# Box-filter layer: all shifted rows copied between the layers, its rings moved, sums and fixes reordered

## The chip, the cores and the metric

The kernel runs on one core of a Trainium2 chip. The metric is the time of one execution on the device in microseconds (us), the median over several executions.

## What is computed

The input is 8 images of 16 channels and 512 x 512 pixels (float32). Two residual layers follow each other; `_gn` normalises over groups of two channels.

```python
# layer 0
x = x + _L0_conv_ref(_gn(x), w_real, w_imag, b_real, b_imag)   # rfftn, 3x3 complex convolution over the spectrum, irfftn
# layer 1
x = x + _L1_conv_ref(_gn(x))                                   # mean filter 15 x 15, zero padding
```

## The kernel before

One image lies in SBUF as `img`, 128 partitions x 64 rows x 512 pixels. A partition holds one channel (16) and one block of 64 neighbouring rows (8 blocks), so `T` is 64 and step `u` or `t` of a loop treats one row of every block at once. The images follow each other; for each, layer 0 runs over 64 steps, a gap of a few us follows in which the statistics of layer 0's result are made (`statistics`: BN_AGGR, two tiny matmuls, square root, then a chain of one-column operations in `sc`), and then layer 1 runs over 64 steps, storing its rows and loading those of the next image. From step 16 on (`follow`, `LAG`) layer 1 also counts and sums the rows of the next image; the last image has nothing to follow.

Layer 1 filters 15 rows by a running sum. POOL writes the difference of the entering and the leaving row (`difference`, L1490), ACT scales it (`scale_row`, L946 or L947), PE turns it by a transposition that accumulates nothing (`turn_step`, L759), ACT and DVE split the turned row into two float16 parts (`high_part` L812, `low_part` L1343), PE multiplies them with a band matrix that adds into one PSUM bank (`box_row`, L770), and DVE adds the bank to the image row (`add_box`, L1351) into `ob_all`, which has three buffers of two rows. SP stores a buffer (L371); `add_box` of an even row waits until the store that used the buffer three pairs earlier has landed. The first filter row is made from `head` and `tail` (`turn_first`): `tail` is the sum of the last rows of each block, added up by POOL (`presum`, L1442 and L1445), scaled by DVE (L1356) after the statistics.

The blocks lie in different partitions, so the rows across a block's edge have to be moved between partitions by DMA on SP's queue, seven rows before a block (`rows_before`) and seven after it (`rows_after`). Before, both sets share the pieces 4 to 10 of one buffer, `arena`: the rows before are copied in the gap, the rows after, in two parts, in layer 1 itself, behind the stores of pair 0 and pair 2. The differences of steps 8 to 56 go through a ring of three rows (`diff`), the float16 parts through another (`parts`), both in `arena` too. POOL's first difference waits for `tail_ready`, the scaled tail.

At the end of layer 0, POOL finishes row 63's two additions (`add_terms`, L1430 and L1433), DVE adds them to the image (`finish_row`, L1281, then BN_STATS, L1284), ACT makes the half mean (L878) and adds it to the row (L888), and DVE corrects all 64 row means in one operation (L1334) before BN_AGGR (L1122).

Each engine works through its own program in order; the order is written by hand and held by semaphores. The wait of `add_box` for a store is this:

```python
if u % 2 == 0:
    dve.wait_ge(stored[j % NS], PRIMED + 32 * (b * USES[j % NS] + j // NS))
```

Of the kernel before, what the change touches and what calls it, by code (L numbers as in the profile page):

```python
# [32 lines left out]
F16 = mybir.dt.float16  # L33
# [128 lines left out]
def build(nc, x, w_real, w_imag, b_real, b_imag, tab, bd_dram, out):  # L162
    x_v = x.rearrange("b c (s hl t) w -> b s c hl (t w)", s=2, hl=HL)
    out_v = out.rearrange("b c (s hl t) w -> b s c hl (t w)", s=2, hl=HL)
    with ExitStack() as ctx:
# [21 lines left out]
        diff = [piece[s] for s in (0, 1, 11)]  # L187
        parts = [piece[s].bitcast(F16).rearrange("p (l k m) -> p l k m", l=2, k=NQ) for s in (2, 3, 12)]
        head, tail = piece[14], piece[15]
        across = [piece[4 + r] for r in range(R)]  # L190
        across_all = arena[:, 4 * W:(4 + R) * W]

        def diff_row(u):
            return across[u - 1] if u <= R else diff[u % 3] if u < T - R else across[u - (T - R)]
# [24 lines left out]
        wrap_row = sb("wrap_row", [P, W], F16)  # L219
        wrap_high = sb("wrap_high", [P, W], F16)  # L220
        block_mat = sb("block_mat", [P, 9, P])
        kappa = sb("kappa", [P, 3, T, 2])
        bias_c = sb("bias_c", [P, 2, T, 2])
# [65 lines left out]
        before_in, after_in = [[sem(f"{name}{s}") for s in range(2)] for name in ("before_in", "after_in")]  # L289
# [52 lines left out]
        def _(sp):  # L342
# [93 lines left out]
            def rows_before(b):  # L436

                def shifted(first, rows, signal):
                    to, at = across_all[:, first * W:(first + rows) * W], T - R + first
                    of = img[:, at:at + rows, :].rearrange("p t w -> p (t w)")  # L440
# [4 lines left out]
                sp.dma_start(across_all[0:HP:HL], tab["no_row"]).then_inc(before_in[0], 16)  # L445
                sp.wait_ge(x1_whole, (b + 1) * T - 3)
                shifted(0, 4, before_in[0])
                sp.wait_ge(x1_whole, (b + 1) * T)
                shifted(4, 3, before_in[1])

            def rows_after(b, part):

                first, rows = ((0, CHUNK), (CHUNK, R - CHUNK))[part]
                to = across_all[:, first * W:(first + rows) * W]
                of = img[:, first:first + rows, :].rearrange("p t w -> p (t w)")
                sp.wait_ge(turned, b * T + first + rows + 1)
                for hl in range(HL - 1):
                    sp.dma_start(to[hl:P:HL], of[hl + 1:P:HL]).then_inc(after_in[part], 16)
                sp.dma_start(to[HL - 1:HP:HL], of[HP:P:HL]).then_inc(after_in[part], 16)
                sp.dma_start(to[HP + HL - 1:P:HL], tab["no_row"][:, 0:rows * W]).then_inc(after_in[part], 16)  # L460

            with sp.Fori(0, B - 1) as b:
                matrices(b)
                rows_before(b)
                for j in range(T // 2):
# [4 lines left out]
                    if j in (0, 2):  # L470
                        rows_after(b, j // 2)
# [1061 lines left out]
```

## Time and profile before

| | |
|---|---|
| median of 3 runs | 3462.5 us (3455.91 to 3465.9) |
| the profiled execution's own time | 3468.07 us |
| its span, first to last instruction | 3466.0 us |
| mean granted TensorE clock | 0.978 |
| busy: PE, DVE, POOL, ACT | 89%, 89%, 78%, 71% |
| DMA | 573.59 MB, mean 165 GB/s |

PE and DVE are both busy for nine tenths of the span, so an idle stretch of either is a place where the other, or a DMA, is waited for. An image takes 414 us, some 130 us of them in layer 1.

### The profile page before, as it was taken

Reading aid. Unit: us, or ns where it says so; the run is one execution under the profiler, and the core shown is the slowest. Engines: PE = TensorE matmul, PEld = TensorE weight load, DVE = VectorE, ACT = ScalarE, POOL = GpSimd, SP = SyncE. Lnnn points to the kernel's source line nnn. Section 1 sums busy time; section 2 is a strip of 40 time slices with the busy share of each in tenths; the row PEclk is TensorE's granted clock in tenths of the full one; section 3 lists DMA queues with packets and bytes.
Section 4 is the critical chain, followed back from the end, with each engine's and each line's share of the span. In section 5 each row is a group of like instructions: output and inputs, shape, how many; then the busy total and the mean of one; then the engine's idle time right before and its main releaser. Section 6 shows DMA issues by size and latency. Waiting matters only on the chain.

```text
span 3466.0 us, 112555 instructions
## 1 busy us (share of the span) xinstructions
PE 3085.5 (89%) x36064; PEld 1877.5 (54%) x36064; DVE 3077.9 (89%) x6018; ACT 2447.4 (71%) x4742; POOL 2713.3 (78%) x2231
## 2 busy tenths in 40 slices
PE   2299979999889998899899998999989999889986
PEld 1155555555555555555555555555555555555555
DVE  7789978999889989899798997989978998889987
ACT  2568865787658876588666886578865887658876
POOL 5069975899749987599876997589974998749986
PEclk9599999999999999999999999999999999999999
DMA  8656668666776659766596666966678665877655
GB/s 206 202 87 131 129 202 257 114 128 124 241 214 128 127 119 288 170 127 129 155 288 130 130 128 188 276 110 128 121 230 227 122 127 118 261 194 130 127 130 176
DMA packets 726766, 573.59 MB, mean 165 GB/s; under 512 B 592416, under 2 KB 667776, under 8 KB 712064
## 3 DMA queue, kind: packets, MB, share of 16 engines
q1 hardware_dynamic: 704000, 451.67, 56.0%
q10 hardware_dynamic: 22400, 117.46, 13.2%
q8 instruction: 178, 2.92, 0.4%
q14 instruction: 188, 1.54, 0.2%
HBM read 262.08 MB, written 148.90 MB: 119 GB/s over the span
## 4 chain that ended last, share of the span: by engine, by line
PE 43%; DVE 19%; issue 14%; POOL 10%; SPq 7%; DMA 5%; ACT 1%; ACTq 1%; DVEq 1%; POOLq 0%
PE p L626 19%; PE h_ps L536 7%; PE h_odd L536 7%; DVE ob_all L1351 5%; POOL arena L1490 4%; SPq L417 3%; DVE arena L1343 3%; PE p L770 3%; DMA out<-ob_all 3%; PE h_ps L626 2%; DVE stat L1104 2%; POOL ob_all L1433 2%; DVE ob_all L1272 2%; PE p L633 2%; POOL ob_all L1430 2%
## 5 line engine op out<-in xcount | busy, mean ns | idle before, releaser
L626 PE MATMUL p<-arena,bd_all 64*64 64x512 f16 x16896 | 1263.2, 380 | 25.3 <-DVE ob_all L1266 14.2
L626 PEld LDWEIGHTS p<-arena,bd_all 64*64 64x64 f16 x16896 | 556.4, 105 | 435.2 <-issue 281.8
L1430 POOL TENSOR_TENSOR ob_all<-ob_all,img 128x512 f32<-128x512 f32 x512 | 663.6, 1296 | 60.0 <-DVE ob_all L1266 55.3
L1433 POOL TENSOR_TENSOR ob_all<-ob_all 128x512 f32<-128x512 f32 x512 | 653.4, 1276 | 40.1
L1490 POOL TENSOR_TENSOR arena<-img 128x512 f32<-128x512 f32 x392 | 498.3, 1273 | 176.5 <-PE h_ps L759 97.5
L888 ACT ACTIVATE img<-img,half_row (+1 forms) x1024 | 489.0, 531 | 5.1 <-ACT half_row L878 0.4
L770 PE MATMUL p<-band,arena 128*128 128x135 f16 (+1 forms) x4096 | 341.8, 228 | 151.7 <-DVE ob_all L1351 146.2
L1266 DVE SCALAR_TENSOR_TENSOR ob_all<-p,bias_c,cosw 128x256 f32<-128x256 f32 x1024 | 445.9, 477 | 22.3 <-PE p L626 9.1
L1272 DVE SCALAR_TENSOR_TENSOR ob_all<-p,bias_c,cosw 128x256 f32<-128x256 f32 x1024 | 443.8, 475 | 0.0
L1423 POOL TENSOR_TENSOR arena<-arena 128x512 f16<-128x512 f32 x256 | 309.2, 1208 | 162.0 <-ACT arena L862 162.0
L861 ACT ACTIVATE arena<-img,sc 128x512 f16 (+1 forms) x512 | 435.2, 850 | 0.0
L946 ACT ACTIVATE arena<-arena,sc 128x512 f32<-128x512 f32 x392 | 282.8, 721 | 210.0 <-POOL arena L1490 196.2
L1351 DVE SCALAR_TENSOR_TENSOR ob_all<-p,img 128x512 f32<-128x512 f32 x512 | 348.1, 680 | 86.2 <-PE p L770 52.2
L1284 DVE BATCH_NORM_STATS2 stat<-img (+1 forms) x512 | 355.6, 695 | 58.6
L770 PEld LDWEIGHTS p<-band,arena 128*128 128x128 f16 x4096 | 261.9, 99 | 256.3 <-issue 241.7
L536 PE MATMUL h_ps<-hilbert,arena 128*128 128x256 f16 x3072 | 380.0, 274 | 7.1 <-DMA arena<-arena 7.0
L575 PE MATMUL p<-img,bd_all 128*64 128x256 f32 x2048 | 301.9, 404 | 92.5 <-POOL bd_all L1394 66.5
L536 PE MATMUL h_odd<-hilbert,xT_more 128*128 128x256 f16 x3072 | 379.8, 273 | 1.0 <-DMA xT_more<-arena 0.7
L536 PEld LDWEIGHTS h_ps<-hilbert,arena 128*128 128x128 f16 x3072 | 280.2, 98 | 139.8 <-issue 99.4
L536 PEld LDWEIGHTS h_odd<-hilbert,xT_more 128*128 128x128 f16 x3072 | 279.9, 98 | 137.7 <-issue 96.4
L1423 POOL TENSOR_TENSOR arena<-g_more,arena 128x512 f16<-128x512 f32 x256 | 307.5, 1201 | 58.3 <-ACT g_more L862 38.2
L1104 DVE BATCH_NORM_STATS2 stat<-img 128x6 f32<-128x512 f32 x512 | 335.4, 681 | 3.0 <-DMA img<-in_x 1.7
(182 smaller groups left out, 5191.5 us busy)
## 6 DMA issues: line engine op xcount, KB each, us to landing
out<-ob_all SPq DMA_DIRECT2D x512, 256.0 KB, 4.7
bd_all<-bd_dram SPq DMA_DIRECT2D x512, 224.0 KB, 2.5
img<-in_x ACTq DMA_DIRECT2D x168, 512.0 KB, 6.9
img<-in_x ACTq DMA_DIRECT2D x112, 256.0 KB, 5.3
img<-in_x SPq DMA_DIRECT2D x24, 512.0 KB, 25.7
arena<-img SPq DMA_DIRECT2D x48, 256.0 KB, 3.3
arena<-img SPq DMA_DIRECT2D x48, 192.0 KB, 2.6
bd_dram<-ob_all SPq DMA_DIRECT2D x11, 768.0 KB, 3.6
```

The source lines that it names most:

```text
L536: m = mm(dst(a), row[:, 4 * lx + k, :], tb["hilbert16"][:, lt, k, 0:cols], start=(half == 0 and i == 0), stop=(half == 1 and i == 2))
L626: m = mm(bank[out_half * HP:(out_half + 1) * HP, :], bd[s % RB][rows, 6 * lm + (j if own else j + 1), :], part, start=opens and i3 == 0, s ...
L770: m = mm(p0[0][:, lo:hi], parts[u % 3][:, l, k, :], tb["band16"][:, lo - k * P + R:hi - k * P + R], start=(u == 0 and k == 0 and l == 0), ...
L861: nc.scalar.activation(halves(gp[s][:, 0, :]), row, ACT.Identity, bias=sc[:, 9:10], scale=sc[:, 8:9])
L888: ins = nc.scalar.activation(row, row, ACT.Identity, bias=half_row[:, s, a:a + 1])
L1266: ins = V.scalar_tensor_tensor(t1[:, a, :], p1[:, a * HALF:(a + 1) * HALF], bias_c[:, 1, t, 1 - a:2 - a], cosw[:, a, :], ALU.subtract, ALU ...
L1272: ins = V.scalar_tensor_tensor(t2[:, a, :], p2[:, a * HALF:(a + 1) * HALF], bias_c[:, 0, t, 1 - a:2 - a], sinw[:, a, :], ALU.add, ALU.mult)
L1351: V.scalar_tensor_tensor(ob[j % NS][:, u % 2, :], p0[0], 1.0 / (K * K * BOX_SCALE), img[:, u, :], ALU.mult, ALU.add).then_inc(row_out, 1)
L1423: G.tensor_tensor(gp[s][:, 1, :], g32[s % 2], gp[s][:, 0, :], ALU.subtract).then_inc(g_split, 1)
L1430: G.tensor_tensor(q, term_row[s % 2][0], parity(img[:, t, :]), ALU.add).then_inc(first_added, 1)
L1433: G.tensor_tensor(q, q, term_row[s % 2][1], ALU.add).then_inc(q_done, 1)
L1490: G.tensor_tensor(diff_row(u), more, less, ALU.subtract).then_inc(moved, 1)
```

## The change

All 14 shifted rows are now copied in the gap between the layers (`rows_across`): the rows before to pieces 0 to 6 of `arena`, the rows after to pieces 7 to 13. The rings of differences and of parts move out of `arena` into buffers that layer 0 uses: `g32_more`, `xT_more`, `wrap_rows`, a joint buffer of `kappa` and `bias_c`, and `bd_all`. POOL's first difference no longer waits for the scaled tail. POOL adds `presum` of row 60 behind row 63's additions. DVE corrects the means of rows 0 to 59 ahead of `finish_row` of row 63, and those of the last four behind it. Four SCALAR_TENSOR_TENSOR operations on one column in `statistics` become TENSOR_SCALAR with a column as scalar. ACT's `high_part(0)` stands ahead of `scale_row(2)`.

```diff
--- before.py
+++ after.py
@@ -184,14 +184,11 @@
...
 
-        diff = [piece[s] for s in (0, 1, 11)]
-        parts = [piece[s].bitcast(F16).rearrange("p (l k m) -> p l k m", l=2, k=NQ) for s in (2, 3, 12)]
         head, tail = piece[14], piece[15]
-        across = [piece[4 + r] for r in range(R)]
-        across_all = arena[:, 4 * W:(4 + R) * W]
+        rows_of_before, rows_of_after = arena[:, 0:R * W], arena[:, R * W:2 * R * W]
 
         def diff_row(u):
-            return across[u - 1] if u <= R else diff[u % 3] if u < T - R else across[u - (T - R)]
+            return piece[u - 1] if u <= R else diff[u % 3] if u < T - R else piece[R + u - (T - R)]
 
...
@@ -216,11 +213,16 @@
...
-        kappa = sb("kappa", [P, 3, T, 2])
-        bias_c = sb("bias_c", [P, 2, T, 2])
+        biases = sb("biases", [P, 5 * 2 * T])
+        kappa = biases[:, 0:6 * T].rearrange("p (f t a) -> p f t a", f=3, a=2)
+        bias_c = biases[:, 6 * T:10 * T].rearrange("p (f t a) -> p f t a", f=2, a=2)
+        flat16 = bd_all[:].rearrange("p s r -> p (s r)")
+        diff = [g32_more[:], xT_more[:], biases[:, 0:W]]
+        parts = [row.rearrange("p (l k m) -> p l k m", l=2, k=NQ)
+                 for row in (flat16[:, 0:2 * W], flat16[:, 4 * W:6 * W], wrap_rows[:])]
...
@@ -433,51 +435,43 @@
...
-            def rows_before(b):
+            def rows_across(b):
+
+                def rows_of(first, rows):
+                    return img[:, first:first + rows, :].rearrange("p t w -> p (t w)")
 
                 def shifted(first, rows, signal):
-                    to, at = across_all[:, first * W:(first + rows) * W], T - R + first
-                    of = img[:, at:at + rows, :].rearrange("p t w -> p (t w)")
+                    to, of = rows_of_before[:, first * W:(first + rows) * W], rows_of(T - R + first, rows)
                     for hl in range(HL - 1):
                         sp.dma_start(to[hl + 1:P:HL], of[hl:P:HL]).then_inc(signal, 16)
                     sp.dma_start(to[HP:P:HL], of[HL - 1:HP:HL]).then_inc(signal, 16)
                 sp.wait_ge(p0_ready, (b + 1) * T + PRIMED)
-                sp.dma_start(across_all[0:HP:HL], tab["no_row"]).then_inc(before_in[0], 16)
+                sp.dma_start(rows_of_before[0:HP:HL], tab["no_row"]).then_inc(before_in[0], 16)
                 sp.wait_ge(x1_whole, (b + 1) * T - 3)
                 shifted(0, 4, before_in[0])
+                to, of = rows_of_after, rows_of(0, R)
+                for hl in range(HL - 1):
+                    sp.dma_start(to[hl:P:HL], of[hl + 1:P:HL]).then_inc(after_in, 16)
                 sp.wait_ge(x1_whole, (b + 1) * T)
                 shifted(4, 3, before_in[1])
-
-            def rows_after(b, part):
-
-                first, rows = ((0, CHUNK), (CHUNK, R - CHUNK))[part]
-                to = across_all[:, first * W:(first + rows) * W]
-                of = img[:, first:first + rows, :].rearrange("p t w -> p (t w)")
-                sp.wait_ge(turned, b * T + first + rows + 1)
-                for hl in range(HL - 1):
-                    sp.dma_start(to[hl:P:HL], of[hl + 1:P:HL]).then_inc(after_in[part], 16)
-                sp.dma_start(to[HL - 1:HP:HL], of[HP:P:HL]).then_inc(after_in[part], 16)
-                sp.dma_start(to[HP + HL - 1:P:HL], tab["no_row"][:, 0:rows * W]).then_inc(after_in[part], 16)
+                sp.dma_start(to[HL - 1:HP:HL], of[HP:P:HL]).then_inc(after_in, 16)
+                sp.dma_start(to[HP + HL - 1:P:HL], tab["no_row"]).then_inc(after_in, 16)
 
             with sp.Fori(0, B - 1) as b:
                 matrices(b)
-                rows_before(b)
+                rows_across(b)
...
                     store(b, j, j % NS)
-                    if j in (0, 2):
-                        rows_after(b, j // 2)
                     if j == 4:
                         sp.wait_ge(turned, b * T + 1)
                         sp.dma_start(tail, tab["hilbert_kernel"]).then_inc(bias_in, 16)
             matrices(B - 1)
-            rows_before(B - 1)
+            rows_across(B - 1)
             for j in range(T // 2):
                 store(B - 1, j, j % NS)
-                if j in (0, 2):
-                    rows_after(B - 1, j // 2)
             for s in range(NS):
                 sp.wait_ge(stored[s], PRIMED + 32 * B * USES[s])
 
@@ -961,15 +955,15 @@
...
                 scale_row(1)
+                high_part(0)
                 scale_row(2)
-                high_part(0)
                 def load_next(t, rows, signal):
 
                     act.wait_ge(row_out, PRIMED + b * T + t + rows)
                     if t + rows + R <= NDIFF:
                         act.wait_ge(moved, b * NDIFF + t + rows + R)
                     if t < R:
-                        act.wait_ge(after_in[t // CHUNK], (b + 1) * (16 * COPIES))
+                        act.wait_ge(after_in, (b + 1) * (16 * COPIES))
...
@@ -1124,18 +1118,17 @@
                 dve.wait_ge(s_mean, n)
                 V.tensor_copy(sc[:, 6:7], c_ps[:, 16:17])
                 lk(V.tensor_tensor(sc[:, 2:3], sc[:, 0:1], c_ps[:, 16:17], ALU.subtract))
-                V.scalar_tensor_tensor(sc[:, 3:4], sc[:, 2:3], sc[:, 2:3], sc[:, 1:2],
-                                       ALU.mult, ALU.add).then_inc(s_dev, 1)
+                V.tensor_scalar(sc[:, 3:4], sc[:, 2:3], sc[:, 2:3], sc[:, 1:2], ALU.mult, ALU.add).then_inc(s_dev, 1)
                 dve.wait_ge(s_gvar, n)
                 V.tensor_scalar(sc[:, 4:5], c_ps[:, 17:18], EPS, None, ALU.add).then_inc(s_var, 1)
                 dve.wait_ge(s_sd, n)
                 dve.wait_ge(s_var, n)
                 lk(V.reciprocal(sc[:, 7:8], sc[:, 5:6]))
 
-                lk(V.scalar_tensor_tensor(sc[:, 11:12], sc[:, 7:8], sc[:, 7:8], sc[:, 4:5], ALU.mult, ALU.mult))
+                lk(V.tensor_scalar(sc[:, 11:12], sc[:, 7:8], sc[:, 7:8], sc[:, 4:5], ALU.mult, ALU.mult))
                 lk(V.tensor_scalar(sc[:, 11:12], sc[:, 11:12], -0.5, 1.5, ALU.mult, ALU.add))
-                lk(V.scalar_tensor_tensor(sc[:, 8:9], sc[:, 7:8], ROW_SCALE, sc[:, 11:12], ALU.mult, ALU.mult))
-                shift = V.scalar_tensor_tensor(sc[:, 9:10], sc[:, 8:9], -1.0, sc[:, 6:7], ALU.mult, ALU.mult)
+                lk(V.tensor_scalar(sc[:, 8:9], sc[:, 7:8], ROW_SCALE, sc[:, 11:12], ALU.mult, ALU.mult))
+                shift = V.tensor_scalar(sc[:, 9:10], sc[:, 8:9], -1.0, sc[:, 6:7], ALU.mult, ALU.mult)
...
@@ -1328,11 +1321,16 @@
...
                 wave_terms(b * T + T - 1, T - 1, (T - 1) % NG, T // NG)
-                for t in (T - 2, T - 1):
-                    finish_row(b * T + t, t, t % NG, T // NG)
-                dve.wait_ge(half_made, (b + 1) * T)
-                V.scalar_tensor_tensor(parity_mean, parity_mean, 0.5, known[:], ALU.mult, ALU.add).then_inc(stat_fixed, 1)
-                dve.wait_ge(stat_fixed, b + 1)
+                def fix_means(first, end):
+
+                    dve.wait_ge(half_made, b * T + end)
+                    V.scalar_tensor_tensor(parity_mean[:, first:end], parity_mean[:, first:end], 0.5,
+                                           known[:, first:end], ALU.mult, ALU.add).then_inc(stat_fixed, 1)
+                finish_row(b * T + T - 2, T - 2, (T - 2) % NG, T // NG)
+                fix_means(0, T - 4)
+                finish_row(b * T + T - 1, T - 1, (T - 1) % NG, T // NG)
+                fix_means(T - 4, T)
+                dve.wait_ge(stat_fixed, 2 * b + 2)
                 statistics(b * 2 + 2, b, False)
 
...
@@ -1466,9 +1464,8 @@
                         slot(i, s, 1)
                 for t in range(T - NG, T):
                     slot(t // NG, t % NG, t // NG, sum_t=t - 4 if t - 4 >= T - R else None)
-                presum(b * T + T - 4, T - 4)
                 add_terms(b * T + T - 1, T - 1, (T - 1) % NG, T // NG)
-                for t in range(T - 3, T):
+                for t in range(T - 4, T):
                     presum(b * T + t, t)
 
...
@@ -1485,11 +1482,10 @@
                             pool.wait_ge(turned, b * T + u - 2)
                         more, less = img[:, u + R, :], img[:, u - R - 1, :]
                     else:
-                        pool.wait_ge(after_in[0 if u - (T - R) < CHUNK else 1], (b + 1) * (16 * COPIES))
+                        pool.wait_ge(after_in, (b + 1) * (16 * COPIES))
                         more, less = diff_row(u), img[:, u - R - 1, :]
                     G.tensor_tensor(diff_row(u), more, less, ALU.subtract).then_inc(moved, 1)
 
-                pool.wait_ge(tail_ready, b + 1)
                 for u in range(1, T):
                     difference(u)
                     if follow and u >= LAG + 2 and (u - (LAG + 2)) % CHUNK == 0:
```

What stands on SP's queue (between the fetches of layer 0's matrices, L407 before and L409 after, and the stores of layer 1, L371 and L373). Before:

```order
L445 DMA arena<-tab_no_row 16x3584
L442 DMA arena<-img 32x2048 x3
L443 DMA arena<-img 16x2048
L442 DMA arena<-img 32x1536 x3
L443 DMA arena<-img 16x1536
L371 ISA
L371 DMA out<-ob_all 16x4x1024
L371 ISA
L371 DMA out<-ob_all 16x4x1024
L458 DMA arena<-img 32x2048 x3
L459 DMA arena<-img 16x2048
L460 DMA arena<-tab_no_row 16x2048
```

And now:

```order
L449 DMA arena<-tab_no_row 16x3584
L446 DMA arena<-img 32x2048 x3
L447 DMA arena<-img 16x2048
L454 DMA arena<-img 32x3584 x3
L446 DMA arena<-img 32x1536 x3
L447 DMA arena<-img 16x1536
L457 DMA arena<-img 16x3584
L458 DMA arena<-tab_no_row 16x3584
L373 ISA
L373 DMA out<-ob_all 16x4x1024
L373 ISA
L373 DMA out<-ob_all 16x4x1024
```

The rows after a block (L458 to L460 before, L454, L457 and L458 now) stand ahead of the first store instead of between the stores, and three of them stand ahead of the second part of the rows before.

POOL at the end of layer 0 (`add_terms` of rows 62 and 63 and the presums of rows 59 to 63; `arena` is the tail). Before:

```order
L1430 TENSOR_TENSOR ob_all<-ob_all,img 128x512
L1433 TENSOR_TENSOR ob_all<-ob_all 128x512
L1444 ISA
L1445 TENSOR_TENSOR arena<-arena,img 128x512
L1444 REGISTER_ALU
L1445 TENSOR_TENSOR arena<-arena,img 128x512
L1429 REGISTER_ALU
L1430 TENSOR_TENSOR ob_all<-ob_all,img 128x512
L1433 TENSOR_TENSOR ob_all<-ob_all 128x512
```

And now:

```order
L1428 TENSOR_TENSOR ob_all<-ob_all,img 128x512
L1431 TENSOR_TENSOR ob_all<-ob_all 128x512
L1442 ISA
L1443 TENSOR_TENSOR arena<-arena,img 128x512
L1427 REGISTER_ALU
L1428 TENSOR_TENSOR ob_all<-ob_all,img 128x512
L1431 TENSOR_TENSOR ob_all<-ob_all 128x512
```

One presum has moved from ahead of row 63's two additions to behind them.

ACT at the start of layer 1 (the scaled head, then scaled differences 1, 2, 3 and the high parts 0 and 1). Before:

```order
L947 ACTIVATE arena<-arena,sc 128x512
L951 ISA
L947 ACTIVATE arena<-arena,edge_bias,sc 128x512
L951 REGISTER_ALU
L947 ACTIVATE arena<-arena,edge_bias,sc 128x512
L812 ACTIVATE arena<-h_ps 128x512
L951 REGISTER_ALU
L947 ACTIVATE arena<-arena,edge_bias,sc 128x512
L812 ACTIVATE arena<-h_ps 128x512
```

And now:

```order
L941 ACTIVATE arena<-arena,sc 128x512
L945 ISA
L941 ACTIVATE arena<-arena,edge_bias,sc 128x512
L806 ACTIVATE bd_all<-h_ps 128x512
L945 REGISTER_ALU
L941 ACTIVATE arena<-arena,edge_bias,sc 128x512
L945 REGISTER_ALU
L941 ACTIVATE arena<-arena,edge_bias,sc 128x512
L806 ACTIVATE bd_all<-h_ps 128x512
```

Two scalings instead of one stand between high part 0 and high part 1.

## Rows read from the trace of the kernel before

**Rows 1.** Waits of DVE, whole run: us in total, times, longest.

```profile
DVE ob_all L1351 <- DMA out<-ob_all: 33.9, 15, 5.2
```

**Rows 2.** Timeline of DVE, L1351: start, us, operation, [idle before <- releaser].

```profile
464.97 0.68 DVE L1351 SCALAR_TENSOR_TENSOR ob_all<-p,img 128x512 f32<-128x512 f32 x1
...
482.08 0.69 DVE L1351 SCALAR_TENSOR_TENSOR ob_all<-p,img 128x512 f32<-128x512 f32 x1 [0.23 <-PE p L770]
...
487.62 0.69 DVE L1351 SCALAR_TENSOR_TENSOR ob_all<-p,img 128x512 f32<-128x512 f32 x1 [4.24 <-DMA out<-ob_all]
...
494.95 0.67 DVE L1351 SCALAR_TENSOR_TENSOR ob_all<-p,img 128x512 f32<-128x512 f32 x1
...
2966.76 0.69 DVE L1351 SCALAR_TENSOR_TENSOR ob_all<-p,img 128x512 f32<-128x512 f32 x1 [0.24 <-PE p L770]
...
2981.07 0.67 DVE L1351 SCALAR_TENSOR_TENSOR ob_all<-p,img 128x512 f32<-128x512 f32 x1
...
3381.74 0.69 DVE L1351 SCALAR_TENSOR_TENSOR ob_all<-p,img 128x512 f32<-128x512 f32 x1 [0.53 <-DMA out<-ob_all]
```

**Rows 3.** Timeline, DMA issues of SP and of ACT in the first layer 1.

```profile
475.25 2.50 SPq L458 DMA_DIRECT2D arena<-img  x3
...
479.21 4.04 SPq L371 DMA_DIRECT2D out<-ob_all  x4
...
478.09 0.70 ACTq L974 DMA_DIRECT2D img<-in_x  x1
```

**Rows 4.** Windows: stretch, us, busy us of PE, PEld, DVE, ACT, POOL, PEclk, DMA share, GB/s.

```profile
502.00:552.00 50.00, 49.99 (x450) 31.15 (x448) 50.00 (x85) 33.65 (x56) 39.31 (x36) 1.00 1.00 292
```

**Rows 5.** DMA issues from 500 to 556 us: count, KB each, median us to landing.

```profile
out<-ob_all SPq DMA_DIRECT2D x32, 256.0 KB, 5.8
```

**Rows 6.** Timeline of the first gap, from layer 0's last rows to layer 1's first.

```profile
445.15 2.64 POOL L1445 TENSOR_TENSOR arena<-arena,img 128x512 f32<-128x512 f32 x2
...
447.75 1.29 POOL L1430 TENSOR_TENSOR ob_all<-ob_all,img 128x512 f32<-128x512 f32 x1
...
449.12 1.27 POOL L1433 TENSOR_TENSOR ob_all<-ob_all 128x512 f32<-128x512 f32 x1
...
450.42 0.75 DVE L1281 SCALAR_TENSOR_TENSOR img<-p,sc,ob_all 128x512 f32<-128x512 f32 x1 [2.37 <-POOL ob_all L1433]
...
452.44 0.69 DVE L1334 SCALAR_TENSOR_TENSOR stat<-stat,known 128x128 f32<-128x128 f32 x1 [0.55 <-ACT half_row L878]
...
453.18 1.88 DVE L1122 BATCH_NORM_AGGREGATE sc<-stat 128x2 f32<-128x384 f32 x1
...
458.13 0.22 DVE L1145 TENSOR_SCALAR edge_bias<-ends,sc 128x2 f32<-128x2 f32 x1
458.25 0.15 DVE L1146 TENSOR_SCALAR sc<-sc 128x1 f32<-128x1 f32 x1
...
458.57 0.55 DVE L1356 TENSOR_SCALAR arena<-arena,sc 128x512 f32<-128x512 f32 x1
459.28 8.66 POOL L1490 TENSOR_TENSOR arena<-img,arena 128x512 f32<-128x512 f32 x7 [4.38 <-DVE arena L1356]
459.47 0.38 PE L749 MATMUL h_ps<-ident,arena 128*128 128x128 f32 x2
...
462.53 0.58 ACT L812 ACTIVATE arena<-h_ps 128x512 f16<-128x512 f32 x1
...
463.76 0.57 ACT L812 ACTIVATE arena<-h_ps 128x512 f16<-128x512 f32 x1
```

**Rows 7.** DVE's L1210 beside POOL: one pair in the timeline, and the line's ns min/median/max.

```profile
605.44 1.16 POOL L1423 TENSOR_TENSOR arena<-g_more,arena 128x512 f16<-128x512 f32 x1 [2.97 <-DVE img L1204]
605.51 1.11 DVE L1210 TENSOR_SCALAR edge<-edge,sc 128x2 f32<-128x2 f32 x1
...
L1210 DVE TENSOR_SCALAR edge<-edge,sc x8: 228/666/1111, 189.8 to 3091.5; 128x2 f32<-128x2 f32 x8
```

**Rows 8.** The page's DMA issues: count, KB each, median us to landing.

```profile
arena<-img SPq DMA_DIRECT2D x48, 256.0 KB, 3.3
```

More of the change, by code:

```diff
@@ L218, in build @@
         xT = [row.bitcast(F16).rearrange("p (k m) -> p k m", k=8) for row in (piece[9], xT_more[:])]
-        wrap_row = sb("wrap_row", [P, W], F16)
-        wrap_high = sb("wrap_high", [P, W], F16)
+        wrap_rows = sb("wrap_rows", [P, 2 * W], F16)
+        wrap_row, wrap_high = wrap_rows[:, 0:W], wrap_rows[:, W:2 * W]
         block_mat = sb("block_mat", [P, 9, P])
-        kappa = sb("kappa", [P, 3, T, 2])
-        bias_c = sb("bias_c", [P, 2, T, 2])
+        biases = sb("biases", [P, 5 * 2 * T])
[5 more added lines that the diff above has]
+                 for row in (flat16[:, 0:2 * W], flat16[:, 4 * W:6 * W], wrap_rows[:])]
         known = sb("known", [P, T, 2])
@@ L288, in build @@
         scaled_row = sem("scaled_row")
-        before_in, after_in = [[sem(f"{name}{s}") for s in range(2)] for name in ("before_in", "after_in")]
+        before_in, after_in = [sem(f"before_in{s}") for s in range(2)], sem("after_in")
         turned, high_done, low_done, banded = sem("turned"), sem("high_done"), sem("low_done"), sem("banded")
@@ L914, in image @@
                 act.wait_ge(v_stacked, b + 1)
-                nc.scalar.activation(wrap_high[:], p0[2], ACT.Identity, scale=sc[:, 27:28]).then_inc(v_high, 1)
+                nc.scalar.activation(wrap_high, p0[2], ACT.Identity, scale=sc[:, 27:28]).then_inc(v_high, 1)
                 def slot(i, s, first):
@@ L1228, in layer0 @@
                 dve.wait_ge(c_made, b + 1)
-                V.tensor_copy(bias_c[:], c_tab[:, 0:2])
+                V.tensor_copy(bias_c, c_tab[:, 0:2])
                 lk(V.scalar_tensor_tensor(known[:], c_tab[:, 2], unscale, parity_mean, ALU.mult, ALU.add))
@@ L1233, in layer0 @@
                 dve.wait_ge(v_high, b + 1)
-                V.scalar_tensor_tensor(wrap_row[:], p0[2], sc[:, 26:27], wrap_high[:],
+                V.scalar_tensor_tensor(wrap_row, p0[2], sc[:, 26:27], wrap_high,
                                        ALU.mult, ALU.subtract).then_inc(v_wrap, 1)
```

## The prediction

> **What bounds the kernel now.** I read the waits of DVE first, because in layer 1 DVE adds every row and everything else follows its row count. The reader is to see one line there [rows 1]: `add_box` waited 33.9 us in the whole run for a store to land. Then I read where this happens, from the starts of `add_box` [rows 2]. Rows 0 to 11 of the first layer 1 take 482.08 - 464.97 = 17.11 us, 1.555 us a row. Row 12 then starts 5.54 us behind row 11 instead of 1.6, and its bracket says that it waited 4.24 us for `out<-ob_all`. The queues say why [rows 3]: row 12 reuses the buffer of pair 3. That pair was complete when row 7 was, near 476.5, but its store was issued at 479.21, behind the five copies of `rows_after`, part 2, that begin at 475.25; and the first 1 MB load of the next image enters the DMA engines at 478.09. From step 16 on, with the next image's rows counted and summed, PE and DVE are both busy for all of 50 us [rows 4]: there the row takes three DVE operations, no DMA is waited for though the engines move 292 GB/s, and nothing of this change reaches it. The third view is the gap between the layers [rows 6], a single chain from POOL's last additions over DVE's statistics to the first high part.
>
> **The stores' stall.** From row 11 to row 16 the first image takes 494.95 - 482.08 = 12.87 us [rows 2]. Without a wait it would take four steps of 1.555 and one of 1.80, since step 16 has a third DVE operation (three of 0.6): 8.02 us. The excess is 4.85 us: 4.24 of wait, the rest in the slower rows behind it. Seven images have a next image to load, and of the seven the first has the smallest excess and the seventh, with 2981.07 - 2966.76 = 14.31 us, the largest, 6.3. Between them lie 13.80, 12.91, 13.08, 12.88 and 13.00; together the seven excesses make 36.7 us. The eighth image has the same copies and no loads, and waited 0.53 us of which 0.24 is its ordinary pause [rows 2]: 0.3 us. So copies and loads together make the stall, neither the copies alone. The change takes 1.75 MB of copies out of this stretch, and with them the 2.7 us by which store 3 was late. What then stands between store 3 and its landing is the first load. Store and load demand 2 MB in 6.2 us here, 320 to 340 GB/s, more than the 292 of the steady stretch, where a store lands in 5.8 us [rows 4, 5]. The time allowed is from the second issue of a pair's store to the row that reuses it: five rows less 0.7 for the add and 1.4 for the issues, 7.8 - 2.1 = 5.7 us. That is even with 5.8, so I leave a remainder: between 0 and the half of the wait, 2.5 us an image, I take 0.5, as the burst lasts only five rows. Gain: 37.0 - 7 x 0.5 = 33.5 us.
>
> **The gap, ahead of the statistics.** Row 63's additions start directly behind the presum of row 59, at 445.15 + 2.64 / 2 = 446.47, instead of 447.75 [rows 6]: 1.28 us earlier. L1433 then ends at 449.11 and `finish_row` of row 63 could start there instead of at 450.42. But the new correction of 60 means stands in front of it and reads two SBUF operands while POOL works. What such an operation does is seen beside another operation of POOL [rows 7]: L1210, two columns of arithmetic, takes 0.228 us at best and 1.11 here, and 605.51 + 1.11 = 606.62 is where POOL's operation ends, 605.44 + 1.16 = 606.60. It waits until POOL's operation is over. The correction so ends some 0.15 us behind L1433 (an estimate between 0.02 of that pair and the 0.69 of L1334), and `finish_row` starts at 449.29, 1.13 us earlier. Its old successor L1334 came 2.02 us after it; the small correction of four means is due then, at 451.31, and again waits for the presum that POOL is at. POOL's operations follow each other by (8.66 - 1.27) / 6 = 1.23 us [rows 6]; from 449.29 the second ends at 451.8. BN_AGGR starts at 451.97 instead of 453.18: 1.2 us gained.
>
> **The gap, under POOL's differences.** Before, POOL stood idle for 4.38 us until the tail was scaled [rows 6], so no DVE operation of the statistics ever met it. Now presums run to 454.3 and differences 1, 2, 3, 4 start at 454.3, 455.55, 456.8 and 458.05. The four operations on one column cost 0.06 us more each, the difference between a TENSOR_SCALAR with a column as scalar and one without (0.22 against 0.15) [rows 6]: 0.24. L1145, two columns and of exactly L1210's form, is then due at 458.13 - 1.2 + 0.24 = 457.17, in difference 3, waits until 458.05 and ends at 458.23; before it ended at 458.35. The scaled tail L1356 is due at 458.45, in difference 4, and waits until 459.4; it ends near 459.85 where it ended at 459.12. `turn_first` starts 0.73 later than 459.47 and lasts 1.97, so high part 0 can start at 462.17, 0.36 earlier than 462.53. Behind it now stand two scalings instead of one. High to high was 463.76 - 462.53 = 1.23 with one; I take 0.72 for another, so high part 1 starts 1.95 later, at 464.12, 0.36 later than before. The first `add_box` waits for low part 1, so the rows start 0.36 us later: 8 x 0.36 = +2.9 us. Bounds: with no wait for POOL in the statistics the rows would start 1.3 us earlier (-10.6); with a further full operation of 1.23 us they would start 1.6 later (+12.8). I take the computed value, since every wait was placed by its own phase; L1145 would have to come 0.37 us earlier to slip in ahead of difference 3.
>
> The input's statistics run the same four operations, with POOL idle: 8 x 0.24 = +1.9 us.
>
> The Trainium skill, GPSIMD Engine Reference, section 1 (Specifications), says that POOL's SBUF interfaces are shared with VectorE, with contention for VectorE instructions in a two-port mode or with two SBUF inputs. By that rule L1145, L1356 and the corrections wait, and the trace agrees for L1210 (1.11 against 0.228 us). One-column TENSOR_SCALARs would not, if they have nothing to split; no row here shows one beside a busy POOL, and the sum takes them at their idle price.
>
> **The copies in the gap.** They cost nothing by my reckoning, and what hides them is this. The first four rows before lie in front of them on the queue. Three copies of 448 KB follow, then, from 452.2 on, the three other rows before: 1.4 MB and 0.7 MB. A 256 KB copy lands 3.3 us after issue [rows 8]; at the steady 292 GB/s [rows 4] the 2.1 MB take 7.2 us from about 451, so they land near 458.5. Difference 5 needs them at 459.3. If they are later, POOL waits, but scaled difference 5 is not needed by `turn_step` before 467; the cover is 6 to 7 us, and the cost beyond it is one for one. The last two copies, 0.44 MB, are needed at difference 57 and by the first load.
>
> **Sum.** 3468.07 - 33.5 + 2.9 + 1.9 = 3439.4 us for a profiled execution. The one of before stood 5.6 us above its median of 3462.5, so 3433.8; I say 3433.
>
> **The rivals.** First, no waits for POOL in the statistics, or lucky phases: everything else equal, -10.6 instead of +2.9, 3420 us. For it: L1334 in the old gap did pass POOL with only 0.69 us. Against: L1210 [rows 7]. 15%.
>
> Second, the stall is the loads' and not the copies'. Then half of it stays, say 16.5 us: 3450. For it: the burst demands more than the steady stretch, and 5.7 us allowed against 5.8 to land is no margin [rows 5]. Against: in the steady stretch itself no store is waited for, and store 3 was 2.7 us late by the copies alone [rows 3]. 13%.
>
> Third, slower than before. The one-column operations also wait for POOL. The five operations from L1135 to the first of the group with L1145 each wait for the one before, so each would catch POOL's next boundary: 5 x 1.23 = 6.2 us instead of 1.2 of their own, and 0.8 for L1127, 5.8 us an image, 46 us: 3479. It decides above 3.6 us an image, three operations that wait. For it: nothing in the trace shows a one-column operation beside a busy POOL that passes unhindered. Against: they have one tensor operand of one element, and the operations of layer 1 that read one operand from SBUF keep their 0.68 us while POOL works [rows 2]. The Trainium skill, VectorE: DVE Perf Modes, section Mode 2x_2P, says the two-port mode splits an operand in halves; one column has none, which speaks against this rival. 8%.
>
> The forecast keeps 60%; 4% is left for what I have not seen.
>
> **How the numbers follow.** 0.3% is 10 us, about what a measurement here can tell from no change, so faster means under 3452. The forecast and the first rival are faster, 75%, and of the second, centred at 3450, two thirds, 9%: 84%. Same is the other third of the second and half of the unseen, with rounding 8%; slower the third rival, 8%. The range runs from the first rival with a whole stall gained, 3412, to the second, 3452; outside are the third rival and the tails. The forecast's own range, 3424 to 3442, comes from the remainder of the stall (0 to 1.5 us an image) and a shift of the gap by half a POOL operation.
>
> **What would show it.** `add_box`'s wait for `out<-ob_all` falls from 33.9 to under 5 us, and row 11 to row 16 takes 8 to 8.6 us in every image. POOL's first difference starts near 454 and L1145 lasts near 1 us, L1356 over 1 us instead of 0.55. BN_AGGR starts 1.2 us sooner after the last matmul of layer 0, the first `add_box` at about the old time. The prediction is wrong if the wait on the stores stays above 15 us, if one-column TENSOR_SCALARs of the statistics last over 0.5 us in the gap, or if the steady rows change their 1.79 us.

## The result, and the profile after

The changed kernel takes 3433.1 us in the median of 7 runs (3431.01 to 3445.7) against 3462.5 (3455.91 to 3467.77): ratio 0.9927, 95% interval 0.991 to 0.9944. The forecast was 3433. Its profiled execution took 3433.1 us, span 3431.1, 35 us less than the one of before.

The waits of DVE, whole run, of the changed kernel (us in total, times, longest), beside [rows 1]:

```profile
DVE ob_all L1349 <- DMA out<-ob_all: 12.8, 19, 1.6
```

The stores' wait has fallen from 33.9 us to 12.8, but it has not gone. The timeline of DVE in the first layer 1 (start, us, operation, idle before) shows where it is now, beside [rows 2]:

```profile
481.25 0.69 DVE L1349 SCALAR_TENSOR_TENSOR ob_all<-p,img 128x512 f32<-128x512 f32 x1 [0.16 <-PE p L764]
...
482.84 0.69 DVE L1349 SCALAR_TENSOR_TENSOR ob_all<-p,img 128x512 f32<-128x512 f32 x1 [0.31 <-PE p L764]
...
486.46 0.69 DVE L1349 SCALAR_TENSOR_TENSOR ob_all<-p,img 128x512 f32<-128x512 f32 x1 [0.81 <-DMA out<-ob_all]
...
489.79 0.67 DVE L1349 SCALAR_TENSOR_TENSOR ob_all<-p,img 128x512 f32<-128x512 f32 x1
```

Row 12 (482.84) no longer waits; row 14 does, 0.81 us. Row 11 to row 16 takes 8.54 us where it took 12.87. The windows of this layer 1 (stretch, us, busy us of PE, PEld, DVE, ACT, POOL, PEclk, DMA share, GB/s) show that the DMA traffic now comes later, with the loads; from 469 to 475 us the kernel before moved 310 GB/s:

```profile
469.00:475.00 6.00, 4.12 (x48) 3.35 (x47) 4.93 (x8) 4.21 (x7) 2.37 (x2) 1.00 0.55 165
...
481.00:487.00 6.00, 3.91 (x44) 3.04 (x41) 4.48 (x8) 4.69 (x8) 5.40 (x6) 1.00 0.98 322
487.00:493.00 6.00, 4.56 (x50) 3.39 (x50) 5.76 (x11) 4.19 (x8) 4.26 (x5) 1.00 1.02 328
```

In the kernel before, the six us that begin in the stall read:

```profile
487.00:493.00 6.00, 4.15 (x33) 3.60 (x34) 3.87 (x6) 2.37 (x4) 2.10 (x2) 0.72 1.03 344
```

The granted clock (PEclk) of that stretch was 0.72 of full speed, so part of it ran at the lower level; from 481.9 to 487.5 PE had been busy for 1.67 of 5.6 us. Now it is 1.00. Rows 12 and 13 of the kernel before took 1.97 and 2.04 us, and the additions behind them waited 0.68 and 0.75 us for PE; in the eighth image, which has no such stall, the same rows took 1.53 and 1.59. So the old stall cost more than its wait.

The timeline of the gap, beside [rows 6]:

```profile
447.07 1.27 POOL L1431 TENSOR_TENSOR ob_all<-ob_all 128x512 f32<-128x512 f32 x1
447.27 1.23 DVE L1327 SCALAR_TENSOR_TENSOR stat<-stat,known 128x120 f32<-128x120 f32 x1
...
448.40 0.74 DVE L1274 SCALAR_TENSOR_TENSOR img<-p,sc,ob_all 128x512 f32<-128x512 f32 x1
...
451.02 1.88 DVE L1116 BATCH_NORM_AGGREGATE sc<-stat 128x2 f32<-128x384 f32 x1
...
453.59 8.80 POOL L1487 TENSOR_TENSOR arena<-img,arena 128x512 f32<-128x512 f32 x7
453.63 0.27 DVE L1121 TENSOR_SCALAR sc<-sc 128x1 f32<-128x1 f32 x1
...
456.14 1.19 DVE L1138 TENSOR_SCALAR edge_bias<-ends,sc 128x2 f32<-128x2 f32 x1
...
457.55 1.26 DVE L1354 TENSOR_SCALAR arena<-arena,sc 128x512 f32<-128x512 f32 x1
...
461.02 0.60 ACT L806 ACTIVATE bd_all<-h_ps 128x512 f16<-128x512 f32 x1 [2.02 <-PE h_ps L744]
461.52 1.51 ACT L941 ACTIVATE arena<-arena,edge_bias,sc 128x512 f32<-128x512 f32 x2
462.93 0.58 ACT L806 ACTIVATE bd_all<-h_ps 128x512 f16<-128x512 f32 x1
```

Three things are to be seen. POOL's seven differences run back to back from 453.59, so neither part of the shifted rows was late. Two DVE operations beside them, L1138 and L1354, last 1.19 and 1.26 us where the same lasted 0.22 and 0.55 (L1145 and L1356, [rows 6]), while L1121, on one column, lasts 0.27, as it does in the input's statistics with POOL idle. And ACT stands idle for 2.02 us ahead of high part 0 and then needs two scalings before high part 1.

From the starts of BN_AGGR, `finish_row` and `add_box` in the two timelines, summed over the eight images (one profile of each kernel):

| stretch, us | before | after | difference |
|---|---|---|---|
| input's BN_AGGR to row 0 of layer 0 | 259.8 | 254.1 | -5.7 |
| rows 0 to 62 of layer 0 | 1894.3 | 1892.3 | -1.9 |
| row 62 to row 63 | 30.7 | 20.1 | -10.6 |
| row 63 to BN_AGGR | 22.2 | 21.0 | -1.1 |
| BN_AGGR to first row of layer 1 | 95.4 | 105.1 | +9.8 |
| rows 0 to 11 | 136.9 | 136.8 | -0.1 |
| rows 11 to 16 | 100.9 | 70.9 | -30.0 |
| rows 16 to 32 | 225.5 | 229.8 | +4.3 |
| rows 32 to 63, and to the next BN_AGGR | 522.4 | 522.2 | -0.2 |

### The profile page after: what moved, and what is told of

Its sections match the earlier page's. It is cut to its first block, busy times and chain, and to the rows that moved or that the text cites. A ratio compares the mean times of both kernels' runs of the same rounds, so it can differ in the third digit from the quotient of the medians.

```text
span 3431.1 us, 112508 instructions
## 1 busy us (share of the span) xinstructions
PE 3066.6 (89%) x36064; PEld 1863.3 (54%) x36064; DVE 3101.3 (90%) x6026; ACT 2443.8 (71%) x4742; POOL 2712.3 (79%) x2231
## 4 chain that ended last, share of the span: by engine, by line
PE 45%; DVE 24%; issue 11%; POOL 6%; DMA 5%; SPq 4%; ACT 2%; ACTq 1%; DVEq 1%; POOLq 0%
PE p L620 20%; PE h_ps L530 8%; PE h_odd L530 7%; DVE ob_all L1349 7%; DMA out<-ob_all 3%; PE p L764 3%; DVE bd_all L1341 3%; DVE stat L1098 2%; DVE ob_all L1265 2%; SPq L419 2%; PE h_ps L620 2%; PE p L627 2%; POOL ob_all L1431 2%; DVE ob_all L1259 1%; DVE img L1274 1%
## 5 line engine op out<-in xcount | busy, mean ns | idle before, releaser
L1259 DVE SCALAR_TENSOR_TENSOR ob_all<-p,biases,cosw 128x256 f32<-128x256 f32 x1024 | 445.7, 477 | 22.0 <-PE p L620 8.7
L1265 DVE SCALAR_TENSOR_TENSOR ob_all<-p,biases,cosw 128x256 f32<-128x256 f32 x1024 | 443.6, 475 | 0.0
L764 PE MATMUL p<-band,bd_all 128*128 128x135 f16 (+1 forms) x2752 | 225.1, 226 | 89.7 <-DVE ob_all L1349 89.6
L627 PE MATMUL p<-wrap_rows,bd_all 64*64 64x512 f16 x1536 | 299.9, 376 | 0.0
L1274 DVE SCALAR_TENSOR_TENSOR img<-p,sc,ob_all 128x512 f32 (+1 forms) x384 | 285.2, 743 | 0.0
L863 ACT ACTIVATE arena<-h_ps 128x512 f16<-128x512 f32 x256 | 152.9, 597 | 180.2 <-PE h_ps L530 180.2
## 6 DMA issues: line engine op xcount, KB each, us to landing
img<-in_x SPq DMA_DIRECT2D x24, 512.0 KB, 25.7
```

What stands on the lines that cost most here:

```text
L627: m = mm(p0[s % RB][out_half * HP:(out_half + 1) * HP, :], wrap_mat[s % RB][half * HP:(half + 1) * HP, out_half * HP:(out_half + 1) * HP], ...
L1259: ins = V.scalar_tensor_tensor(t1[:, a, :], p1[:, a * HALF:(a + 1) * HALF], bias_c[:, 1, t, 1 - a:2 - a], cosw[:, a, :], ALU.subtract, ALU ...
L1265: ins = V.scalar_tensor_tensor(t2[:, a, :], p2[:, a * HALF:(a + 1) * HALF], bias_c[:, 0, t, 1 - a:2 - a], sinw[:, a, :], ALU.add, ALU.mult)
```

## The experiments

Each kernel is the changed one with one edit, unless it says otherwise. Ratios are to the kernel before, timed on the same chip.

**The changed kernel again.**

> The changed kernel itself once more, to read the others against on the same chip and to see how far its profiles differ. Both theories: ratio to the kernel before within 0.991 to 0.9944 as measured; finish of row 62 to finish of row 63 2.51 us in every image; the waits for landed stores differ from image to image by up to 2 us.

3434.28 us, ratio 0.9917 (0.9901 to 0.9932). Rows 62 to 63 sum to 20.0 us again and BN_AGGR to first row to 105.2. Rows 11 to 16 sum to 72.6 (70.9), rows 16 to 32 to 228.6 (229.8), the input's BN_AGGR to row 0 to 255.3. So the gap repeats to 0.1 us over the run, and the burst and the parts of layer 0 to some 2 us.

**Copies back into layer 1.**

```diff
-                to, of = rows_of_after, rows_of(0, R)
-                for hl in range(HL - 1): ...
+            def rows_after(first, rows): ...          # five copies, then_inc(after_in, 16)
                     store(b, j, j % NS)
+                    if j in (0, 2):
+                        rows_after(*((0, 4), (4, 3))[j // 2])
-                        act.wait_ge(after_in, (b + 1) * (16 * COPIES))
+                        act.wait_ge(after_in, (b + 1) * (32 * COPIES))
```

> The changed kernel with one thing put back: the rows after a block are copied in layer 1 again, in two parts behind the stores of pairs 0 and 2 (to their new place, so nothing else moves). Theory (the copies make the stall): rows 11 to 16 go from 8.9 us on average back to 12.5 to 13.5 in the seven images that load, the waits for a landed store from 12.8 to over 30 us, time 25 to 33 us above the changed kernel, about 3460. Rival (the loads' burst makes it, and the change gained elsewhere): at most 8 us above the changed kernel, waits for stores under 18 us.

3461.13 us, ratio 0.999 (0.9979 to 1.0): the whole gain is gone. But the trace does not show what the theory said. Rows 11 to 16 sum to 72.5 us, as in the changed kernel; it is rows 0 to 11 that grew, by 25.0 us, and the waits for landed stores are 6.2 us, not over 30. ACT's timeline says why:

```profile
478.21 1.73 ACTq L975 DMA_DIRECT2D img<-in_x  x2
480.06 0.72 ACT L947 ACTIVATE biases<-biases,sc 128x512 f32<-128x512 f32 x1 [4.92 <-issue]
```

ACT stood 4.92 us ahead of its next scaling: my edit left one semaphore for all 14 rows, so the first load, issued by ACT in its order, waited for the second part of the copies (its last copy landed at 478.05, the load was issued at 478.21), and everything behind it on ACT with it. The time fits the theory, and the cause is another one. It was therefore made again.

**Copies back, a semaphore for each part.**

```diff
+            def rows_after(part): ...                 # then_inc(after_in[part], 16)
-                        act.wait_ge(after_in, (b + 1) * (16 * COPIES))
+                        act.wait_ge(after_in[t // CHUNK], (b + 1) * (16 * COPIES))
```

> As the first experiment (rows after copied in layer 1 again, behind the stores of pairs 0 and 2, to their new place), but with a semaphore for each part, so that the first load waits only for the first part, as before the change. Theory (the copies and the loads together keep the stores of pairs 3 and later from landing): ACT no longer stands for the load at row 8 to 11, rows 0 to 11 take 17.1 us, rows 11 to 16 12.8 to 14.3, the waits for landed stores are over 30 us, and the time is 25 to 33 us above the changed kernel. Rival (the semaphore for all 14 rows made the first experiment slow, the copies themselves cost little): less than 8 us above the changed kernel.

3463.13 us, ratio 1.0003 (0.9992 to 1.0014), against 3434.6 on the same chip for the kernel with the loads in halves (below), which times like the changed one. Rows 0 to 11 sum to 136.8, rows 11 to 16 to 101.4 us, and the wait is where it was before (waits of DVE; then its timeline, idle before in brackets):

```profile
DVE ob_all L1357 <- DMA out<-ob_all: 35.4, 13, 5.3
```

```profile
480.25 0.69 DVE L1357 SCALAR_TENSOR_TENSOR ob_all<-p,img 128x512 f32<-128x512 f32 x1 [0.23 <-PE p L772]
485.99 0.69 DVE L1357 SCALAR_TENSOR_TENSOR ob_all<-p,img 128x512 f32<-128x512 f32 x1 [4.44 <-DMA out<-ob_all]
```

The eighth image, which has these copies and no load, takes 7.83 us for the same rows, as without them. The copies, together with the loads, make the stall; moving them is what the change gains.

**The Hilbert row's load out of the burst.**

```diff
-                    if j == 4:
+                    if j == 24:
```

> The changed kernel with the 256 KB load of the Hilbert row issued after the store of pair 24 instead of pair 4, out of the burst of stores and first loads. Theory (what is left of the stall is the DMA engines' load, the Hilbert row's quarter of a megabyte in it): the waits for landed stores fall from 12.8 to 4 to 8 us, rows 11 to 16 from 8.9 us to 8.1 to 8.4; 4 to 8 us faster than the changed kernel. Rival (the two loads of 1 MB alone keep the stores late): less than 2 us faster.

3436.81 us, ratio 0.9912 (0.9896 to 0.9928); waits 11.4 us, rows 11 to 16 71.4 us. The rival holds: the Hilbert row does not make what is left of the waits.

**Loads in halves.**

```diff
-                        if u % CHUNK == CHUNK - 1 and 0 <= k < NCH - LAG // CHUNK:
-                            load_next(k * CHUNK, CHUNK, loaded[k])
+                        if u % 2 == 1 and 0 <= k < NCH - LAG // CHUNK:
+                            load_next(k * CHUNK, CHUNK, loaded[k], (u % CHUNK // 2,))
```

> The changed kernel with each 1 MB load of four rows issued as one half at steps 9, 13, ... and the other at steps 11, 15, ..., so that the burst from step 11 on is spread. Theory (what is left of the stores' wait is the megabyte that enters at once): waits for landed stores fall from 13 us to 3 to 7, rows 11 to 16 to 8.0 to 8.4 us, 5 to 9 us faster than the changed kernel. Rival (the remainder is the mean demand of loads and stores at 1.55 us a row, whatever its grain): waits 10 to 16 us as now, time within 3 us of the changed kernel.

3434.6 us, ratio 0.9921 (0.9905 to 0.9938); waits 12.6 us, rows 11 to 16 76.3 us, more than the 70.9 and 72.6 of the changed kernel. In time the rival holds. But the waits have moved: all 12.6 us lie in rows 12 to 16 and none behind them, where the two profiles of the changed kernel have 2.9 and 3.1 us behind row 32, and the stretch from row 32 to the next BN_AGGR sums to 517.3 us instead of 522. The edit also issues the first half two rows earlier, so it shows that smaller loads gain nothing in all, and not that their grain is without effect.

**The one-column operations as SCALAR_TENSOR_TENSOR again.**

```diff
-                lk(V.tensor_scalar(sc[:, 8:9], sc[:, 7:8], ROW_SCALE, sc[:, 11:12], ALU.mult, ALU.mult))
+                lk(V.scalar_tensor_tensor(sc[:, 8:9], sc[:, 7:8], ROW_SCALE, sc[:, 11:12], ALU.mult, ALU.mult))
```

> The changed kernel with the four one-column TENSOR_SCALARs of the statistics as SCALAR_TENSOR_TENSOR again (three SBUF operands, two of them tensors). Theory (two SBUF inputs wait for POOL): each of the four, in the gap alone, lasts until POOL's running difference ends, up to 1.2 us instead of 0.2 to 0.27; the gap grows by 2 to 4 us, in all 15 to 30 us slower than the changed kernel, less the 2 us that the input's statistics win. Rival (an operation on one column is too small to wait): 2 to 4 us faster, since the SCALAR_TENSOR_TENSORs are 0.05 us shorter.

3478.41 us, ratio 1.004 (1.0021 to 1.0059): slower than the kernel before. Its timeline in the first gap:

```profile
450.21 1.24 DVE L1121 SCALAR_TENSOR_TENSOR sc<-sc 128x1 f32<-128x1 f32 x1
...
452.55 0.22 DVE L1129 SCALAR_TENSOR_TENSOR sc<-sc 128x1 f32<-128x1 f32 x1
...
452.99 0.93 DVE L1131 SCALAR_TENSOR_TENSOR sc<-sc 128x1 f32<-128x1 f32 x1
453.96 1.19 DVE L1132 SCALAR_TENSOR_TENSOR sc<-sc 128x1 f32<-128x1 f32 x1
```

Three of the four wait for POOL; L1129 met the joint between two differences. BN_AGGR to first row grows from 105.2 to 134.9 us, 3.7 an image, as expected. The time does not fit as well: the ratio is 1.2% above the changed kernel's, 43 us, where at most 28 were expected, and the profiled execution, 3466.42, is 33 above; where the other executions lost 10 us more is not shown.

**POOL's wait for the tail, ahead of difference 1, and ahead of difference 3.**

```diff
+                pool.wait_ge(tail_ready, b + 1)       # first kernel
                 for u in range(1, T):
+                    if u == 3:                        # second kernel, instead
+                        pool.wait_ge(tail_ready, b + 1)
                     difference(u)
```

> The changed kernel with POOL's wait for the scaled tail put back in front of its first difference. Theory (VectorE operations with two columns or more from SBUF wait until POOL's running operation ends): with POOL idle, edge_bias lasts 0.22 us again instead of 1.19 and the tail's scaling 0.55 instead of 1.26, the first transposition of layer 1 starts 1.4 us earlier, and as differences 2 and 3 are only needed by then, the rows start about 1.0 us earlier in each image: 8 us faster than the changed kernel. Rival (the early differences are what the change is worth in the gap): the rows start 1.5 to 3 us later in each image, 12 to 24 us slower.

3428.48 us, ratio 0.9896 (0.9878 to 0.9913), 5.8 us less than the changed kernel on the same chip; BN_AGGR to first row 95.7 us instead of 105.2. The theory holds.

> The changed kernel with POOL's wait for the scaled tail in front of difference 3 instead of nowhere, so that differences 1 and 2 are made under the statistics and POOL is idle when edge_bias and the tail are due. Theory: edge_bias 0.22 us, tail 0.55, the first rows 1.5 us earlier than in the changed kernel and 0.5 earlier than with the wait ahead of difference 1; 10 to 13 us faster than the changed kernel. Rival (by then ACT's order of scalings and high parts binds, not POOL): the same as with the wait ahead of difference 1, 6 to 8 us faster.

3419.78 us, ratio 0.9876 (0.9857 to 0.9894); BN_AGGR to first row 92.5 us. The two lines that waited in the changed kernel, in this one (ns, min/median/max):

```profile
L1138 DVE TENSOR_SCALAR edge_bias<-ends,sc x8: 219/220/221, 452.9 to 3304.4; 128x2 f32<-128x2 f32 x8
```

```profile
L1354 DVE TENSOR_SCALAR arena<-arena,sc x8: 545/547/547, 453.3 to 3304.9; 128x512 f32<-128x512 f32 x8
```

The theory holds here too. Letting POOL start at once cost more than it gave: the early differences stood in the way of two DVE operations on the path.

**Two columns as one and one.**

```diff
-                V.tensor_scalar(edge_bias[:], tb["ends"][:], sc[:, 9:10], ...)
+                for i in range(2):
+                    V.tensor_scalar(edge_bias[:, i:i + 1], tb["ends"][:, i:i + 1], sc[:, 9:10], ...)
```

> The changed kernel with edge_bias, two columns, made by two operations of one column each. Theory (one column takes no second port and does not wait, two columns do): each lasts 0.2 us beside the busy POOL where the one lasted 1.19, s_scale comes 0.9 us earlier, the tail's scaling then ends at the boundary of the difference before, 1.2 us earlier; rows start 0.9 to 1.2 us earlier, 7 to 9 us faster. Rival (the wait is for POOL by any operation with a pointer scalar and a tensor from SBUF at that place): each of the two waits, same time or slower by up to 10 us.

3431.14 us, ratio 0.99 (0.9883 to 0.9917). POOL works beside them as before:

```profile
L1139 DVE TENSOR_SCALAR edge_bias<-ends,sc x16: 203/204/206, 452.9 to 3317.8; 128x1 f32<-128x1 f32 x16
```

Never more than 0.206 us, and BN_AGGR to first row 95.4 us: 9.8 less. In the whole run 6 to 9 us of it are seen (ratio 0.99 against the 0.9917 and 0.9927 of the changed kernel), in a spread of 11. The same arithmetic waits with two columns and does not with one.

**The presum ahead of row 63 again.**

```diff
+                presum(b * T + T - 4, T - 4)
                 add_terms(b * T + T - 1, T - 1, (T - 1) % NG, T // NG)
-                for t in range(T - 4, T):
+                for t in range(T - 3, T):
```

> The changed kernel with POOL's presum of row 60 back ahead of row 63's two additions. Theory (row 63's additions are on the path): row 62 to row 63 is 3.8 us again instead of 2.51 in every image, all 8 to 11 us slower than the changed kernel. Rival (the statistics then meet POOL at a better moment and get it back): within 4 us of the changed kernel, with the gap from BN_AGGR to the first row shorter by what row 63 lost.

3448.35 us, ratio 0.9948 (0.9929 to 0.9966). Row 62 to 63 sums to 30.7 us instead of 20.0; the gap behind it gives 1.3 us back. By the ratios the kernel is 7 to 11 us slower than the changed one. The rival falls.

**Halves and the wait ahead of difference 3 together.**

> The half loads and POOL's wait for the tail in front of difference 3 together. Theory: the two gains are in different stretches and add, 3410 to 3416 us, 0.985 to 0.987 of the kernel before. Rival (the half loads gain nothing, or the rows that start earlier meet the loads again): as with the wait in front of difference 3 alone, 0.9876.

3418.51 us, ratio 0.9872 (0.9853 to 0.989): as with the wait alone. The halves add nothing in all: rows 11 to 16 lose 3.8 us against the wait alone, and the stretch from row 32 to the next BN_AGGR gains 4.8.

**Scaling 2 ahead of high part 0, with the wait ahead of difference 3.**

```diff
                 scale_row(1)
-                high_part(0)
                 scale_row(2)
+                high_part(0)
```

> The kernel with the wait in front of difference 3, and ACT's scale_row(2) ahead of high_part(0) again, as before the change. Theory (ACT idles 2 us for the first transposition with difference 2 ready, so the scaling is free there and costs 0.72 us behind high part 0): BN_AGGR to first row 10.8 to 10.9 us instead of 11.57, 5 to 6 us faster than with the wait alone, 0.986 of the kernel before. Rival (the scaling ahead delays high part 0): the same or 1 to 6 us slower.

3415.76 us, ratio 0.9851 (0.983 to 0.9872), the lowest here, though its interval overlaps that of the wait alone. Its first gap, ACT:

```profile
448.70 1.50 ACT L941 ACTIVATE arena<-arena,edge_bias,sc 128x512 f32<-128x512 f32 x2
450.94 0.60 ACT L806 ACTIVATE bd_all<-h_ps 128x512 f16<-128x512 f32 x1 [0.73 <-PE h_ps L744]
451.43 0.80 ACT L941 ACTIVATE arena<-arena,edge_bias,sc 128x512 f32<-128x512 f32 x1
452.14 0.59 ACT L806 ACTIVATE bd_all<-h_ps 128x512 f16<-128x512 f32 x1
```

High part 1 follows high part 0 by 1.20 us, where the changed kernel needs 1.91, and BN_AGGR to first row is 86.9 us instead of 92.5, the same in every image.

## Why the prediction was right

**The stall** was the copies' and the loads' together, as forecast: with the copies back it returns whole. The landing of the stores shows how. In the kernel before, the second store of pair 3 was issued 3.1 to 4.5 us behind its row and landed 7.2 to 8.3 us after issue in the seven images that load; in the eighth it was issued as late, 3.9 us, landed after 3.5, and row 12 waited 0.5 us. The term was mis-sized, and it is the failed step of the sum. I took a remainder of 0.5 us an image, 3.5 in all, since "the burst lasts only five rows" and since the 5.7 us allowed were even with the 5.8 that a store takes in the steady stretch. Measured are 12.8 us of waits, 10.0 of them by row 32; rows 11 to 16 gained 30.0 us and 4.3 were given back by row 32, 25.7 instead of 33.5. In the burst the second store of pair 4 landed 6.5 to 7.5 us after issue, 6.7 in the median of the seven images, and not 5.8, so row 14 waits in every one of them, and rows 16, 18 and 22 in some. Two of the signs that I gave failed with it: the wait did not fall under 5 us, and rows 11 to 16 took 8.4 to 10.3 us in the seven images, not 8 to 8.6. Neither the Hilbert row's 256 KB nor, in all, the size of the loads makes this remainder; that it is the mean demand of stores and loads is what is left, argued and not shown.

**Ahead of the statistics** 1.32 us were gained at row 63 and 0.14 behind it, 1.46 an image where I had 1.2: the large correction ended with POOL's operation and delayed `finish_row` by hardly anything. -11.7 us instead of -9.6; the experiment with the presum puts it on the order of POOL's queue.

**Under POOL's differences** I had computed that two operations wait for POOL, and they do, in every image: 1.19 to 1.32 and 1.26 us. BN_AGGR to first row was to become 11.79 + 1.20 + 0.36 = 13.35 us and became 13.14 in the mean, +9.8 us instead of +12.5, since it had been 12.15 and not 11.79 in three images of the kernel before. Both steps in it are shown: the wait (removed by idling POOL, by splitting the columns, and multiplied by two-input operations), and ACT's order, 0.70 us an image. The one-column rival falls: 0.14 to 0.27 us beside a busy POOL. So does what spoke for the first rival: L1334 in the old gap did not pass POOL with its 0.69 us. It started at 452.44 and ended at 453.13, and POOL's presum ended at 452.95.

The Trainium skill's rule (GPSIMD Engine Reference, section 1), that two-port modes and two SBUF inputs contend, fits the seven forms seen here: TENSOR_SCALAR on 2 and 512 columns and SCALAR_TENSOR_TENSOR with two inputs from SBUF on 1, 8 and 120 columns end with POOL's operation or at most 0.3 us behind it, and TENSOR_SCALAR on one column and BN_AGGR last as long as with POOL idle.

**The copies in the gap** were hidden, as said.

**The sum.** The net of the three terms is -25.7 - 11.7 + 9.8 = -27.6 us, where I had -33.5 - 9.6 + 12.5 = -30.6, and 1.9 for the input's statistics, -28.7. Those operations did get slower, by 0.22 us an image, but their stretch shows no loss: it took 5.7 us less than before. The medians gained 29.4 us. The profiled execution gained 35; 7.6 of it lie in the input's statistics and in layer 0's rows, where the profiles of one kernel already differ by some us (254.1 and 255.3), and what they depend on stays open. That the forecast median came out exact is luck: the stall gave 7.8 us less than I had, the other three terms between them some 7 more. It rests besides on the 5.6 us that I took off because the profiled execution of before stood above its median; the changed kernel's does not.

## What to carry to other kernels

Before work is started earlier on one engine, look at what the other does then: POOL's early start cost DVE two waits of a whole POOL operation, and starting two of its operations early and then holding it gave 12.6 us in the gap over the full early start. When DMA traffic is moved out of a burst, compare the landing time with the time that the buffer allows; if they are even, part of the wait stays; and take the landing time from a stretch as loaded as the one in question (6.7 us here, not the 5.8 of the steady stretch). An experiment whose time fits still has to be read: a merged semaphore made the right number from the wrong cause.

## What the runs showed of the hardware

A DVE operation on a single column, even with two pointer scalars, runs beside a busy POOL in 0.14 to 0.27 us; with two columns it lasts until POOL's operation ends (1.19 us instead of 0.22), and so does a SCALAR_TENSOR_TENSOR on one column with two tensors from SBUF (0.93 to 1.35 us instead of 0.16 to 0.22; 0.22 where it met the joint of two POOL operations). A BN_AGGR of 384 elements did not wait (1.88 us, with POOL idle and beside it). With the copies out of the way the stores and loads moved 322 to 328 GB/s for 12 us, and stores still held an addition up by up to 1.6 us: 256 KB stores landed 6.1 to 7.5 us after issue beside the first load, and 3.0 us in the eighth image, which has no loads. Behind the old stall, in which PE had been idle most of the time, the granted clock was 0.72 over six us and rows took up to 2.04 us instead of 1.59.
